# GpSimd in place of VectorE writes the additive adjacency masks of the first attention

## The reference

```
x = x + L0_gnn(layernorm(x), adj, ...)      # the first attention is in here
x = x + L0_ffn(layernorm(x), ...)           # product with signs and absolute values
x = x + L1_gnn(layernorm(x), adj, ...)      # the second attention, same adjacency
x = x + L1_ffn(layernorm(x), ...)           # product-key lookup, 8 heads, causal attention

# in L0_gnn, after h = h_in @ W_att:
e   = h @ a_att[:F] + (h @ a_att[F:]).T     # 2048 x 2048, a column plus a row
att = softmax(where(adj > 0, e, -9e15), axis=1)
h_prime = att @ h
```

## Time and profile before

| what | value |
|---|---|
| runs | 3: 3891.78, 3929.8, 3938.99 us |
| median | 3929.8 us |
| span of the profiled execution, first to last instruction | 2859.2 us |
| own time of the profiled execution | not recorded apart from the runs; median less span is 1070.6 us |
| DVE busy | 83% |
| POOL busy | 69% |
| PE busy | 56% |
| ACT busy | 26% |
| mean granted TensorE clock | 0.702 |

### The profile page before, as it was taken

How to read it: one execution, slowest core, us unless ns; L and a number is a source line. 1 busy time by engine, 2 the same in 40 slices (tenths; PEclk the granted TensorE clock), 3 DMA queues, 4 the chain that set the end, 5 groups by cost and what they waited for, 6 DMA issues and landing times. The chain is left out here.

```text
span 2859.2 us, 31735 instructions
## 1 busy us (share of the span) xinstructions
PE 1591.0 (56%) x7362; PEld 1220.4 (43%) x7362; DVE 2373.7 (83%) x8263; ACT 744.9 (26%) x1904; POOL 1959.6 (69%) x2064
## 2 busy tenths in 40 slices
PE   6858545664556445554556455554555445554555
PEld 6848434453344334442344234442344333442444
DVE  6689899998888888887888888887888888887874
ACT  5746412231122112221122112221122112221212
POOL 0003777777777777777777777777777777777775
PEclk8969756785578557775677557775678557775678
DMA  4201233333333333333333333333333333333333
GB/s 158 102 1 34 86 103 105 109 107 105 105 108 106 107 105 108 105 106 106 106 108 106 106 105 108 105 107 105 105 108 106 107 105 108 105 107 106 106 105 90
DMA packets 109551, 291.44 MB, mean 102 GB/s; under 512 B 34128, under 2 KB 41808, under 8 KB 107344
## 3 DMA queue, kind: packets, MB, share of 16 engines
q0 software_dynamic: 98304, 268.57, 32.1%
q1 hardware_dynamic: 10080, 20.97, 2.1%
q10 hardware_dynamic: 1008, 0.33, 0.0%
HBM read 288.69 MB, written 1.05 MB: 101 GB/s over the span
## 5 line engine op out<-in xcount | busy, mean ns | idle before, releaser
L288 POOL DMA_INDIRECT ring<-table,rows x2048 | 1952.1, 953 | 714.4 <-issue 587.9
L755 DVE SCALAR_TENSOR_TENSOR ps<-ring,wgt,ps 128x256 f32<-128x256 f32 x1792 | 865.6, 483 | 316.7 <-DMA ring<-table,rows 290.2
L1608 PE MATMUL ps<-ident,work 128*128 128x128 f32 x1088 | 260.2, 399 | 526.7 <-PEq L1601 526.7
L1608 PEld LDWEIGHTS ps<-ident,work 128*128 128x128 f32 x1088 | 201.4, 211 | 581.9 <-issue 581.8
L1622 PE MATMUL ps<-s2w,work 128*128 128x128 f32 x2176 | 418.7, 358 | 35.2 <-PEq L1620 34.4
L1622 PEld LDWEIGHTS ps<-s2w,work 128*128 128x128 f32 x2176 | 381.0, 265 | 84.5 <-issue 82.0
L1590 PE MATMUL ps<-work,qT 128*128 128x512 f32 (+3 forms) x576 | 310.7, 680 | 69.3 <-PEq L1582 64.8
L1296 ACT ACTIVATE s2w<-ps 128x512 f32<-128x512 f32 (+2 forms) x320 | 168.7, 533 | 332.2 <-ACTq L1295 331.8
L1286 ACT ACTIVATE work<-ps,nmax 128x128 f32<-128x128 f32 (+15 forms) x128 | 149.3, 1167 | 318.7 <-ACTq L1284 318.7
L1577 PE MATMUL ps<-ident,work 128*128 128x128 f32 x128 | 46.8, 366 | 316.9 <-PEq L1575 316.9
L1590 PEld LDWEIGHTS ps<-work,qT 128*128 128x128 f32 x576 | 124.9, 238 | 200.0 <-issue 200.0
(11 more groups left out here) (241 smaller groups left out, 2654.3 us busy)
## 6 DMA issues: line engine op xcount, KB each, us to landing
ring<-table,rows POOLq DMA_INDIRECT x2048, 2.7
staged<-adj_in SPq DMA_DIRECT2D x16, 1024.0 KB, 4.8
xs<-x_in SPq DMA_DIRECT2D x4, 256.0 KB, 6.3
wpkq<-w_pkq SPq DMA_DIRECT2D x8, 128.0 KB
out<-xs SPq DMA_DIRECT2D x1, 832.0 KB, 4.4
keyd<-pk_keys SPq DMA_DIRECT2D x16, 32.0 KB
wo<-w_o SPq DMA_DIRECT2D x8, 64.0 KB
out<-xs SPq DMA_DIRECT2D x1, 192.0 KB, 2.1
```

The lines of the kernel that those rows point to most:

```text
L288: nc.gpsimd.indirect_dma_start(ring[:, t % RING, k, :], None, table_d, bass.IndirectOffsetOnAxis(ap=rows[:, t % RING, k:k + 1], axis=0),). ...
L755: return v.scalar_tensor_tensor(out, row, w, acc_ps, ALU.mult, ALU.add)
L1608: ins = m.transpose(ps[:, 2 + (parity + b) % 2, j % 4 * P:(j % 4 + 1) * P], prob[:, t % 2, j * P:(j + 1) * P], ident[:, :])
```

## The change

POOL makes all 16 masks, in a loop of its own between its constants and its bias additions, each as soon as its adjacency tile has landed. DVE no longer does; it waits for `mask_ok`. SP reloads a slot when POOL, not DVE, has read it. The instruction is the same one with the same operands.

```
-        staged_free, dve_done = sem("staged_free"), sem("dve_done")
+        mask_ok, dve_done = sem("mask_ok"), sem("dve_done")
@@ SP
-                    sp.wait_ge(staged_free, t - 2)
+                    sp.wait_ge(mask_ok, t - 2)
@@ POOL, after the constants, before the bias additions
+            for t in range(T):
+
+                pool.wait_ge(in_adj[t % 3], 16 * (t // 3 + 1))
+                nc.gpsimd.tensor_scalar(maskb[:, t, :], staged[:, t % 3, :], 0.0, MASK_FILL, ALU.is_le, ALU.mult).then_inc(mask_ok, 1)
+
@@ DVE, masked(0, t)
-                    dve.wait_ge(in_adj[t % 3], 16 * (t // 3 + 1))
-                    v.tensor_scalar(maskb[:, t, :], staged[:, t % 3, :], 0.0, MASK_FILL, ALU.is_le, ALU.mult).then_inc(dve_done, c.one())
-                    dve.wait_ge(dve_done, c.n)
-                    dve.sem_inc(staged_free, 1)
+                    dve.wait_ge(mask_ok, t + 1)
```

## The result

The changed kernel takes 3985.83 us in the median of five runs (3976.86 to 4025.64) against 3919.3 of five before (3884.25 to 3938.99): 66.5 us more by the medians, and a ratio of 1.020 with a 95% interval of 1.015 to 1.025. It is slower, though whether by more than 2% the interval leaves open. I had forecast 3964 us, 34 more than the median of 3929.8 that I had then.

The account below looks back on a forecast made before the run. PE was taken to bound the first attention and DVE's small instructions, with ACT and PE, the opening. Conversions holding DVE (35.2 us) less the first mask (1.4) gave +33.8 us on 3929.8, so 3964 us, range 3918 to 4015.

Parts of the forecast that it names:

- The span: Whole execution: of the median of 3929.8 us, 1070.6 lie outside the profiled span of 2859.2 and are untouched.
- What bounds the stage: First attention: PE sets the pace at 5.32 us a tile, hiding DVE's masks except the first, worth 1.42 us.
- rival A: First attention: DVE, not PE, sets the pace, so all masks are gained, 24.2 us, giving 3906 us; chance 0.03.
- POOL's masks come: POOL, from the first tile's landing: 3.2 us a conversion, 51 us for 16; bounds 1.8 to 8.2 us.
- Is the mask ever late?: First attention: POOL finishes masks before DVE asks for them, so the new wait costs nothing.
- POOL beside DVE: Opening: DVE's two-input or scalar SBUF instructions wait to the end of a POOL conversion under way, 3.2 us each.
- Eleven of sixteen: Opening: 11 of 16 conversions hold DVE up, 35.2 us, the other five hidden by waits; bounds 0 and 48 us.
- The attention's slack: First attention: DVE has 1.9 us of slack a tile and few conversions are left, so held additions cost 0.
- Rival C: Opening and first attention: conversions of 6 us or more, PE starves; at 8.2 us about 105 us, 4035; chance 0.12.
- Rival B: Opening: DVE gets through between conversions or they are short, -1.4 to +12 us, 3928 to 3942; chance 0.27.

Follow-up runs that it names:

- Experiment 9: The kernel before, with DVE making its first mask in the opening, ahead of its wait for ACT's squares; ratio 1.002 (0.998 to 1.005).
- experiment 4: The kernel before, with nine forms of the 128 x 2048 conversion run once each on POOL behind the last gather; compare and mult took 7.08 to 7.11 us.
- experiment 2: The kernel before, masks still on DVE, plus 16 conversions on POOL that nothing uses, from the first adjacency tile's landing; 4060.34 us in one run.
- experiment 3: The kernel before, plus 120 memsets of 128 x 1024 on POOL from the first adjacency tile's landing; 3959.73 us in one run.
- experiment 5: The changed kernel, with POOL's conversion written as mult and add in place of compare and mult; ratio 0.999 (0.995 to 1.003).
- experiment 7: The kernel before, but POOL makes seven masks (3, 5, ... 15) after the opening with compare and mult, DVE the other nine; ratio 1.005 (0.999 to 1.011).

## Why the prediction was right, and where its numbers were not

The time lies within the range (3918 to 4015) and on the side forecast. The likeliest value was half of what came: +33.8 against +66.5 by the medians. That it fell into the range is in part luck. The forecast stood on a conversion of 2.5 to 5.2 us, and this condition failed. The range's upper part came from 11 conversions of 5.2 us, which by the sum is 3929.8 + 57 - 1.4 = 3985 us; what came were conversions of 7.08 us that held DVE for nine conversions' worth, with waits that gave 6.7 us back. With the count of 11 the measured size would have made +76.5.

*The span.* The 1070.6 us of the sum are no time outside the span; this cost nothing, since I set the gain and loss against the median.

*What bounds the stage.* Right. PE sets the pace of the first attention; with 15 masks less on DVE the stage became no shorter, and rival A is out. Experiment 9 prices the one mask on the path at 1.4 us at the first addition, my 1.42.

*POOL's masks come.* This is the term that was mis-sized: 3.2 us a tile by the affine select, 7.08 measured. The select was no kin to it; the upper bound, the two-input addition times four, gave 5.2 to 8.2 and would have been the better row. The conversions were to end near 75 us and the first addition to begin there; they came at 132.8 and 99.56. The estimate from the Trainium skill (GPSIMD Engine Reference, Performance versus the Vector engine), 3.1 us, was as far off. In experiment 4 no form takes that time: mult with add and a cast are faster, 1.9 us, and the others slower, 5.4 to 7.1.

*Is the mask ever late?* At 7.08 us it is still not, in the changed kernel: the conversions end at 132.8 and the last is needed later than before. With the opening 57 us late, DVE never overtakes POOL.

*POOL beside DVE.* The mechanism is right and experiment 2 shows it by itself. "Held to its end" is right for scalar instructions only. L376 at 56.57 was held to the conversion's end at 58.9, but L371, with two inputs, came free after 4.34 us and ended 4.5 us behind the conversion's start at 51.80, and L374, also with two inputs, ran in 0.28 us in the middle of that conversion. L400, L411, L423 and L429 too ended 4.5 us into a conversion, whenever they had begun. The Trainium skill (SBUF — State Buffer, Who interferes with whom; the words that I quoted stand in its summary for kernel authors) has the second one block until the first finishes, and a two-input instruction contend only with a POOL instruction that reads. The latter is what experiment 3 shows. With the former the trace agrees for scalar instructions, and not for two-input ones beside a conversion of 7.08 us, which were held for its first 4.4 us or so only; beside the one of 1.90 us (L398 in experiment 5) they too were held to its end.

*Eleven of sixteen.* The count was wrong both ways. Some 11 conversions ran before the first addition, and the durations that grew in the opening, overlapping ones counted once, come to 65 us (26.7 of them in the eight normalizations), nine conversions' worth. Idle time that was there before (3.63 us ahead of L374 and others) gives 6.7 back and the first mask 1.4: 57.2 net. With short ones (experiment 5) the count says 20 us and 4.7 came, for the holds were fewer (eight) and the waits hid half of them. I had taken what the waits hide as a number of conversions, five of 16; in the two kernels it is rather a time that changes little, 6.7 and 5.9 us, which is under one long conversion and over three short ones.

*The attention's slack.* The 0 should have been 4.2 + 3.5 us here, and experiment 7 shows some 26 us where seven conversions fall into this stage.

*Rival C* had a chance of 0.12 and is what happened in kind: a conversion of over 6 us, a time at about 2%, and PE running dry, though here for 2.8 us only. Its price was too high, 0.8 of 16 conversions (91 us at 7.1) against 65. *Rival B* gave the time of the cheap form (8.2 us at the mark, within its -1.4 to +12), though DVE did not get through between the conversions.

## What to carry over

Work moved to an idle engine is free only if that engine is idle in what it shares as well: 19.6 us of DVE's hidden work became 116 us of POOL beside DVE's most serial stretch, and all but some 7 us of the holds fell on the path. Before a form of instruction goes to POOL, time that form; two ways to write one mask took 7.1 and 1.9 us. And where DVE must work beside POOL, look for durations that jump in DVE's row with no idle time in brackets.

## What the runs showed of the hardware

- A scalar operation of POOL over 2048 columns takes 7.08 us with compare and mult, 5.37 with a single compare or mult, 1.90 with mult and add, 1.89 as a cast. The types were varied for compare and mult alone and made no difference there (7.08 to 7.11).
- While POOL converts for 7.08 us, DVE's scalar operations from SBUF to SBUF are held to its end, those with two SBUF inputs until some 4.4 us into it. A reciprocal (0.25 us at 74.50) and a copy out of PSUM (0.62 us at 64.43) that begin inside a conversion are not held. Beside a conversion of 1.90 us both kinds are held to its end. Beside POOL's memsets, two-input operations are not held at all (2293 ns as before).
- Executions of the same gathers differ: 2623 us in one profile, 3664 in the next, with nothing else changed. What sets this stays open.
